# Layer 0's last two closings: the first output half is projected ahead of the sums of squares, and the second half gets banks of its own

## What is computed

```
h   = sigmoid(r) * 0.5*(wkv(k, v) + reversed wkv)      # layer 0, k, v, r = projections of gn(x)
h   = (h - mean_c(h)) * rsqrt(var_c(h) + 1e-5) * ln_g + ln_b
out = h @ Wo.T                                          # 192 -> 192 channels
x   = x + out
# layer 1: group norm, layer norm, input projection, two convolutions and
# selective scans (forward, backward), gate, output projection, residual
```

## Time and profile before

| | |
|---|---|
| median of 3 runs | 19161.96 us (19159.08 to 19168.01) |
| the profiled execution | 19135.61 us, of which the span is 19133.8 us |
| busy: DVE (VectorE), POOL, PE (TensorE), ACT (ScalarE) | 90%, 88%, 80%, 69% |
| mean granted clock of TensorE | 0.885 |

### The profile page before, as it was taken

One profiled execution on the slowest core, in us unless ns is written; L12 is line 12 of the kernel. 1 busy time (PEld: TensorE's weight loads), 2 busy tenths in 40 slices (PEclk: granted clock), 3 DMA queues, 4 the chain that ended last, 5 costly groups with the idle time before them and its releaser, 6 DMA issues. The chain is left out here.

```text
span 19133.8 us, 189246 instructions
## 1 busy us (share of the span) xinstructions
PE 15370.5 (80%) x45152; PEld 5349.5 (28%) x45152; DVE 17219.0 (90%) x13583; ACT 13164.2 (69%) x33157; POOL 16897.2 (88%) x11028
## 2 busy tenths in 40 slices
PE   7888878878888788887888778887788878888778
PEld 2222222222222222222222222222222222222222
DVE  7989989899898998989989899898998989989899
ACT  6767767677676776767767677676776767767676
POOL 6979979799797997979979799797997979979799
PEclk8888888888888898888888888888888988888888
DMA  2424424244242442424424244242442424424244
GB/s 73 120 61 112 119 66 118 59 113 118 68 117 60 113 117 68 117 62 115 113 68 118 65 114 109 68 120 65 113 109 68 120 66 114 107 68 120 68 116 104
DMA packets 880283, 1820.18 MB, mean 95 GB/s; under 512 B 189530, under 2 KB 594804, under 8 KB 879028
## 3 DMA queue, kind: packets, MB, share of 16 engines
q1 hardware_dynamic: 879028, 1806.77, 37.6%
HBM read 1083.46 MB, written 245.63 MB: 69 GB/s over the span
## 5 line engine op out<-in xcount | busy, mean ns | idle before, releaser
L1159 DVE TENSOR_TENSOR_SCAN arena<-ps,arena 128x897 f32<-128x897 f32 x5376 | 10985.9, 2064 | 477.9 <-ACT arena L1311 225.4
L1363 POOL TENSOR_TENSOR arena<-arena 128x896 f32<-128x896 f32 x5376 | 9417.5, 1770 | 225.5 <-DVE arena L1159 210.1
L1294 ACT ACTIVATE ps<-arena,A 128x448 f32<-128x448 f32 x10752 | 6390.8, 627 | 2400.0 <-DVE arena L1159 2318.3
L1065 PE MATMUL ps<-arena,rep 128*64 128x448 f32 x21504 | 5506.2, 642 | 1605.0 <-POOL arena L1363 1596.4
L1355 POOL TENSOR_TENSOR arena<-arena 128x896 f32<-128x896 f32 x2688 | 4772.4, 1775 | 210.0 <-DMA arena<-arena 137.5
L1065 PEld LDWEIGHTS ps<-arena,rep 128*64 128x64 f32 x21504 | 1483.1, 154 | 5247.2 <-POOL arena L1363 2835.9
L1148 DVE TENSOR_TENSOR arena<-ps,arena 128x896 f32<-128x896 f32 x2688 | 2862.7, 1065 | 75.4 <-PE ps L985 59.8
L1018 PE MATMUL ps<-arena,diag 128*128 128x448 f32 x5248 | 2193.6, 562 | 77.1 <-DVE arena L1122 77.1
L1057 PE MATMUL ps<-arena,skipd 128*128 128x448 f32 x1344 | 797.0, 679 | 711.6 <-DVE arena L1135 588.3
L1018 PEld LDWEIGHTS ps<-arena,diag 128*128 128x128 f32 x5248 | 985.3, 195 | 1265.5 <-issue 1041.7
L1344 POOL TENSOR_TENSOR arena<-arena 128x448 f32<-128x448 f32 x672 | 656.9, 982 | 512.8 <-DVE arena L1128 512.8
(11 more groups left out here) (171 smaller groups left out, 18878.1 us busy)
## 6 DMA issues: line engine op xcount, KB each, us to landing
arena<-bc_rows SPq DMA_DIRECT2D x3584, 224.0 KB, 4.6
arena<-arena SPq DMA_DIRECT2D x4160, 112.0 KB, 3.6
x_projected<-arena SPq DMA_DIRECT2D x112, 672.0 KB, 3.6
y_forward<-arena SPq DMA_DIRECT2D x112, 672.0 KB, 5.6
arena<-x_projected SPq DMA_DIRECT2D x112, 672.0 KB, 4.8
arena<-y_forward SPq DMA_DIRECT2D x112, 672.0 KB, 6.2
x<-in_x SPq DMA_DIRECT2D x119, 336.0 KB, 3.6
x_normed<-arena SPq DMA_DIRECT2D x112, 336.0 KB, 5.1
```

The lines of the kernel that those rows point to most:

```text
L1065: m = e.matmul(ps[64 * h:64 * h + 64, YBANK, 0:T], rep[:, 0:64], pr[:, (q - 1 + h) % NPR, a * T:a * T + T], start=False, stop=p == NP - 1 ...
L1159: e.tensor_tensor_scan(rev(hh[:, q % NH, 0:W2], s), rev(decays(q)[:, 0:W2], s), rev(bb[:, q % NB, 0:W2], s), car[:, 2 * k + p % 2, n:n + 1 ...
L1294: e.activation(two(decays(q))[:, a, :], dt2[:, r % NR2, p % 2, :], ACT.Exp, scale=Am[s][:, 2 * k + p % 2, n:n + 1]).then_inc(c_ex, 1)
L1363: e.tensor_tensor(pr[:, q % NPR, :].rearrange("p (a b) -> p a b", a=2), two(hh[:, q % NH, :]), cr[:, p - p % 2:p - p % 2 + 2, :], ALU.mult ...
```

## The change

Three edits in closings 5 and 6, and one in the filler:

- the due times of `o` go from 24.3 and 24.5 to 24.1 and 24.3; with `vr` at 24.2 the order on TensorE becomes `o` (k = 0), `vr`, `o` (k = 1)
- half 1 gets banks KB and VB in place of (2, 3)
- half 1 of closings 5 and 6 waits for `b_rs` at 5 (the sums of 3 and 4 have been read) in place of `b_t`
- the filler at the end writes bank 6 in place of 4, and waits for `b_t` at 4 in place of `b_rs` at 5

```diff
     BANKS = {MID: (JB, JB, JB), MID + 1: (JB, JB, (2, 3)), MID + 2: ((KB, VB), JB, JB),
-             MID + 3: ((0, 1), (2, 3), (2, 3))}
+             MID + 3: ((0, 1), (2, 3), (KB, VB))}
...
-            MID + 3: dict(mA=23.5, mM=23.6, hc=23.81, sq=23.9, vr=24.2, rs=24.3, o0=24.3, o1=24.5)}
+            MID + 3: dict(mA=23.5, mM=23.6, hc=23.81, sq=23.9, vr=24.2, rs=24.3, o0=24.1, o1=24.3)}
...
-                        if s >= MID + 2 and k:
+                        if s == MID + 2 and k:
                             w.wait_ge(b_t, LAST.index((m, 0)) + 1)
+                        if s == MID + 3 and k:
+                            w.wait_ge(b_rs, 5)
...
-        w.wait_ge(b_rs, 5)
-        busy(e, 6, KB)
+        w.wait_ge(b_t, 4)
+        busy(e, 6, JB[0])
```

## The result

The changed kernel takes 19218.42 us (median of 11 runs, 19201.85 to 19229.47); the kernel before took 19168.28 us in the same rounds (11 runs, 19149.35 to 19187.43). The ratio is 1.0025 with a 95% interval of 1.0015 to 1.0034: slower by 50 us. The profiled execution took 19201.85 us, span 19200.1 us, mean granted clock of TensorE 0.883.

What follows compares the result with a forecast made beforehand. It took layer 0's tail as bound by two chains meeting at `t` of half 0: squares, sums and 1/sqrt, and VectorE's own list. Later start plus clock fall, 16 x 3.2 = 51 us on 19162, gave 19213 us, range 19168 to 19232.

Steps and rivals of the forecast that it cites:

- slower by over 0.2%: Whole kernel: measured time more than 0.2%, or 38 us, above the kernel before; chance 0.57.
- `o0` ahead of the sums: TensorE, layer 0's tail: projecting half 0 first starts the sums 2.60 us later; waiting for its bank costs at most 0.1 us.
- `t` of half 0: VectorE, layer 0's tail: the scaled copies wait for 1/sqrt, making `t` of half 1 start 1.15 us later.
- The own banks: TensorE, layer 0's tail: half 1 no longer waits 0.71 us; only 0.17 us was on the path, contained in the 1.15.
- First sum: End of layer 0: layer 1 starts 1.0 us later in each of 16 images, +16 us.
- The clock falls in the gap: TensorE, layer 0 to layer 1: a 3.2 us gap between full-width matmuls halves the clock; 3.4 us an image in place of 1.0.
- The count of gaps: Whole trace: gaps of 3.0 to 3.3 us beginning at full clock, 62 with a fall, 39 without; fall put at two to one.
- Second sum: Start of layer 1: later start and clock fall together take 3.2 us in each of 16 images, +51 us.
- the text's own sign: First 5 us of layer 1: clock about 0.5; the prediction is wrong if the clock holds.
- Rival A: Start of layer 1: the clock holds, leaving only the later start, +16 us, 19178 us; chance 0.30.
- Rival B: Layer 0's tail: TensorE had been waiting for the squares, so 3 us faster, 19159 us; chance 0.07 together with layer 1 gains.
- Rival C: Layer 1 up to the first chunk's projections: slow clock lasts, 6.6 us an image, 106 us, 19268 us; chance 0.06.

Runs made afterwards that it cites:

- e4: Kernel before with only the order changed: half 0 of closings 5 and 6 projected ahead of their sums, old banks; 19208.40 us against 19161.14 (1.0023).
- e1: Changed kernel with the old order, sums ahead of both halves, keeping new banks, waits and filler; 19152.32 us against 19161.14 for the kernel before (0.9996).
- e3: Kernel before with 3 filler matmuls in place of 6 at the end of layer 0; 19215.62 us against 19161.14 (1.0029).
- the second trace: Changed kernel run and traced once more, unchanged; 19217.24 us in a single execution.
- e2: Changed kernel with 8 filler matmuls in place of 6 at the end of layer 0; 19231.88 us against 19161.14 for the kernel before (1.0035).
- e8: Kernel before with 7 filler matmuls in place of 6 at the end of layer 0; 19182.08 us against 19148.03 (1.0016).
- e6: Kernel before with 8 filler matmuls in place of 6 at the end of layer 0; 19206.14 us against 19142.71 (1.0039).
- e7: Changed kernel with the old order, closing 6's half 0 statistics behind `t` of half 1, 5 fillers; 19133.58 us against 19148.03 for the kernel before (0.9993).

## Why the prediction was right, and where not

The time was forecast at 19213 us and came out at 19218.42; slower by over 0.2% was the likeliest case. That the two agree to 5 us is in part luck: the clock's share is smaller than forecast, and a loss that the sum did not have makes up for it. Point by point:

- **`o0` ahead of the sums puts 2.60 us in front of them.** Right: the wait for L694 grew by 2.60 us to 4.31 (forecast about 4.3), and no wait for L573 appeared.
- **`t` of half 0 waits for the 1/sqrt, 1.2 us.** Right: 1.84 us after the statistics' start in place of 0.56, +1.28. From those statistics to L625 it is 8.45 us in place of 7.23, +1.22 where 1.15 was forecast. e4 shows the wait without the banks, e1 shows it gone with the old order.
- **The own banks are worth 0.17 us.** Right in the old order: 0.21 in e1.
- **First sum, +1.0 us an image.** Right as a delay: L352 follows L625 by 0.85 us in place of 1.04, and 1.22 - 0.19 = 1.03.
- **The clock falls in the gap.** Right as a mechanism in the first trace: 13 of 16 images have a start of 6.6 to 8.1 us. Where it fell for good, L1098 comes 8.0 us after L625, and L352 to L1098 takes 2.4 us more: 1.03 + 2.4 = 3.4 later, the full price of the text. e3 shows that a gap alone does it.
- **The count of gaps, 62 with a fall and 39 without.** It does not come out of the trace. Between the end of one matmul record and the start of the next I find 32 gaps of 3.0 to 3.3 us that begin at the full level, 16 with a fall by their end and 16 without. Two to one for the fall had less behind it than the text says.
- **Second sum, 16 x 3.2.** This is the term that was wrong inside. "It should be nearly all or none" failed: the second trace had 5 falls of 16, so the start is 0.5 us an image longer than before, where 2.2 was forecast (1.7 in the first trace), at 19217.24 us. By the text's own sign, that the clock must not hold, the prediction failed in 11 images of that trace. What the runs show in place of 3.2 us: layer 1's first subtraction comes 2.9 us an image later in the first trace and 1.7 in the second, and another 0.6 and 1.0 us go between the 24th and the 32nd scan of layer 1, a loss that the sum did not have at all. Together that is 56 and 44 us.
- **e2, the test of that term.** It took the fall away in 15 of 16 images, and the kernel stayed 71 us slower than before. The first subtraction came 1.8 us earlier than in the first trace of the changed kernel, and 1.1 us of it went again between the 24th and the 32nd scan, where the slow groups rose from 7 to 14; in the second traces it is 0.7 and 0.5. Some 26 us of the total of e2 stay without a place.
- **Rival A** (clock holds, +16 us) was priced by a shift that costs only itself. e8 and e6, where the clock holds and only the start is later, refute the price: 34 us for 10 and 63 us for 21. **Rival B** and the gains: nothing of it. **Rival C**, the slow clock further into layer 1, had the right kind of loss at the wrong place: not in the first chain but some 120 us in.

How far the slow group of the third chunk explains the price of a later start: inside every trace the images that have it are about 2.2 us longer there, and the kernels with many of them lose most there. That e4, with 5 slow groups, is as slow as the others, and e7, with 7, the fastest, does not speak against it: e4's layer 1 starts 2.2 us later by itself, e7's 0.9 us earlier. But no experiment removed the group, so it is an association and not shown as the cause. Not settled either: why the group falls in 15 of 16 images at a start 0.65 us later (e8) and in 5 at one 2.2 us later (e4). The fillers added in e6 and e8 were not varied apart from the start; e3, with fewer of them, and e4, with as many as before, are slow as well.

## What to carry to other kernels

A wait that an engine shows is not the bottleneck of a chain: TensorE's 0.71 us came from being early, and the projection moved to fill it stood ahead of the sums that the rest of the chain needs. Before moving work ahead of a step, compare when that step's inputs are ready with when its engine is free; if the engine is the later one, the whole moved work is added to that step (2.60 us here), and what the next engine had to spare is all that is taken off (1.2 us were left here). And a stage whose clock level changes by itself need not pay a shift one for one: test a small delay by itself before pricing a gain or loss at its front.

## What was not expected of the hardware

With the same program, the clock was down at the start of layer 1 in 13 images of one execution and 5 of another, while their times lay 15 us apart. Removing the slow stretch with two more filler matmuls saved its 2.4 us there and nothing in the total (1.0035 against 1.0025, intervals overlapping). A delay of 0.65 us an image, 10 us in sum, cost 34 us by medians (13 to 48 by the interval), while one of 2.2 us, 35 us in sum, cost 47 (29 to 61).
